# Last attention block: five score banks instead of three, and VectorE adds its running sum from key tile 4 on

## The reference, cut to what matters

```python
def _L0_xattn_ref(kv, q, Wq, bq, Wk, bk, Wv, bv, Wo, bo):   # q: 4096 x 512, kv: 3202 x 512, 16 heads of 32
    ...
    scores = jnp.einsum('bhqd,bhkd->bhqk', qh, kh) * scale
    mask = jnp.arange(Lkv)[None, :] <= jnp.arange(Lq)[:, None]
    scores = jnp.where(mask[None, None], scores, -jnp.inf)
    attn = jax.nn.softmax(scores, axis=-1)
    out = jnp.einsum('bhqk,bhkd->bhqd', attn, vh)
    ...
    return out @ Wo.T + bo
...
x = x + _L0_xattn_ref(ctx_1024, _layernorm(x, axis=-1), ...)
x = x + _L0_ffn_ref(_layernorm(x, axis=-1), ...)
```

## Time and profile before

| | |
|---|---|
| median of 3 runs | 2925.99 us (2920.41 to 2928.67) |
| the profiled execution | 2921.6 us, of which the span of the profile is 2920.0 us |
| granted TensorE clock over the span | 0.981 |
| PE busy | 2830.9 us, 97% |
| DVE busy | 1871.1 us, 64% |
| ACT busy | 1522.3 us, 52% |
| POOL busy | 1427.7 us, 49% |
| software DMA queue (POOL's) | 226.77 MB, 33.0% of 16 engines |

### The profile page before, as it was taken

The page is one execution under the profiler, slowest core; times in us unless marked ns, Lnnn a source line. Parts: engine busy times, 40 slices in busy tenths (PEclk is TensorE's granted clock), DMA queues, the critical chain, the costliest instruction groups (busy, mean ns, idle before and its releaser), DMA issues. The chain is left out here.

```text
span 2920.0 us, 42983 instructions
## 1 busy us (share of the span) xinstructions
PE 2830.9 (97%) x15944; PEld 1669.4 (57%) x15944; DVE 1871.1 (64%) x3483; ACT 1522.3 (52%) x2904; POOL 1427.7 (49%) x657
## 2 busy tenths in 40 slices
PE   8989999999999999999999999999898999999996
PEld 7877555554555554555554555553486566556653
DVE  4467888885778775778775778870463544444544
ACT  3232456666566666566667566666424434444332
POOL 0000266778566778566778566778671201111110
PEclk9998899999999999999999999999999999999998
DMA  6558456668746678746668746667694100111000
GB/s 241 189 192 250 120 142 148 148 152 187 181 131 151 157 159 190 183 129 154 154 157 191 172 128 142 142 160 190 172 331 137 58 15 30 44 44 44 30 29 15
DMA packets 138711, 407.95 MB, mean 140 GB/s; under 512 B 11632, under 2 KB 28528, under 8 KB 111888
## 3 DMA queue, kind: packets, MB, share of 16 engines
q0 software_dynamic: 32272, 226.77, 33.0%
q1 hardware_dynamic: 101056, 169.07, 20.1%
q10 hardware_dynamic: 5184, 9.44, 1.0%
HBM read 114.33 MB, written 70.78 MB: 63 GB/s over the span
## 5 line engine op out<-in xcount | busy, mean ns | idle before, releaser
L1046 ACT ACTIVATE pT<-s_bank 128x512 f32<-128x512 f32 (+5 forms) x2176 | 1086.7, 578 | 647.9 <-PE s_bank L1215 470.5
L1063 DVE TENSOR_REDUCE row_max<-m_bank 128x1 f32<-128x512 f32 (+4 forms) x2240 | 1254.1, 624 | 265.5 <-PE m_bank L1168 173.0
L986 POOL TENSOR_TENSOR part_sum<-part_sum,pT 128x2048 f32<-128x2048 f32 x192 | 889.0, 4630 | 121.2 <-ACT pT L1046 116.7
L1215 PE MATMUL s_bank<-q_sb,k_sb 104*128 104x512 f32 (+3 forms) x2176 | 839.1, 411 | 11.6 <-ACT pT L1046 7.6
L1168 PE MATMUL m_bank<-k_sb,q_sb 96*128 96x512 f32 (+4 forms) x2240 | 843.0, 410 | 7.5 <-POOL max_terms L958 2.5
L1168 PEld LDWEIGHTS m_bank<-k_sb,q_sb 96*128 96x128 f32 x2240 | 432.4, 196 | 204.8 <-DVE row_max L1063 126.5
L1215 PEld LDWEIGHTS s_bank<-q_sb,k_sb 104*128 104x128 f32 x2176 | 410.3, 192 | 208.2 <-ACT pT L1046 122.5
L1232 PE MATMUL o_bank<-pT,v_sb 128*32 128x512 f32 (+5 forms) x4352 | 499.0, 576 | 0.0
L986 POOL TENSOR_TENSOR part_sum<-pT 128x2048 f32<-128x2048 f32 x28 | 127.7, 4560 | 304.6 <-ACT pT L1046 156.8
L1232 PEld LDWEIGHTS o_bank<-pT,v_sb 128*32 128x32 f32 (+1 forms) x4352 | 113.4, 110 | 229.9 <-ACT pT L1046 115.2
L1641 POOL TENSOR_TENSOR f_var_eps<-f_mean_var,eps 128x4 f32<-128x4 f32 x8 | 1.6, 202 | 473.8 <-DVE f_mean_var L1860 473.8
(11 more groups left out here) (198 smaller groups left out, 3423.7 us busy)
## 6 DMA issues: line engine op xcount, KB each, us to landing
moved_sum<-pT POOLq DMA_DIRECT2D x208, 1024.0 KB, 7.4
q_sb<-qT_hi SPq DMA_DIRECT2D x64, 256.0 KB, 5.0
k_sb<-kT_hi SPq DMA_DIRECT2D x48, 256.0 KB, 8.3
x_in<-in_x SPq DMA_DIRECT2D x8, 1024.0 KB, 6.1
qT_hi<-q_hi SPq DMA_DIRECT2D x8, 1024.0 KB, 4.2
qT_lo<-q_lo SPq DMA_DIRECT2D x8, 1024.0 KB, 6.5
q_sb<-qT_lo SPq DMA_DIRECT2D x32, 256.0 KB, 4.7
aT<-o_sb ACTq DMA_DIRECT2D x32, 256.0 KB, 5.1
```

The lines of the kernel that those rows point to most:

```text
L986: pool.tensor_tensor(total, pT[:, slot(S - 1), :, q0:] if j and kt == 1 else total, pT[:, slot(S), :, q0:], ALU.add).then_inc(pool_added, 1)
L1046: act.activation(pT[0:rows, slot(S), h, q0:], s_bank[(HG * S + h) % S_RING][0:rows, q0:], ACT.Exp, scale=SCALE).then_inc(exp_done, 1)
L1063: dve.tensor_reduce(row_max[:, j % 2, r, h, c:c + 1], m_bank[p % M_BANKS][:, 0:n], AX_X, ALU.max).then_inc(unit_max, 1)
L1215: mm = pe.matmul(out[:, q0:], k_sb[0:R_END, h, at:at + P], q_sb[query_buffer(g, j)][0:R_END, h, q0:], start=True, stop=kt < 4 * j)
```

## The change

The scores of the last block go round five banks: the three `s_bank`s and two of the maxima's ring, which wait for the last two jobs that used them. From the block's fourth score on a score has no bank to wait for but its own; from the sixth it waits for the Exp of the score five before it. The planner knows of it. `LAST_ADDS` falls from 18 to 4, so that DVE also makes the adds of tiles 5, 7, 9, 11, 13, 15 and 17; POOL keeps those of tiles 1 and 3, the eleven transfers of the block and the multiplication of block 6's output. Nothing is changed in what is moved by DMA, nor in any other block.

```diff
 S_RING, M_BANKS = 3, 4
+LAST_RING = S_RING + 2
...
-LAST_ADDS = 18
+LAST_ADDS = 4
...
+LAST_SCORE = HG * (len(ALL_STEPS) - key_tiles(QB - 1))
+
+
+def score_before(n):
+
+    if n < LAST_SCORE + S_RING:
+        return n - S_RING
+    return n - LAST_RING if n >= LAST_SCORE + LAST_RING else None
...
     def score(self, x, S, h):
-        pe = max(x.pe, x.exp_end[0] + T_TO_WRITE) + turn + self.score_time(j, kt)
+        before = score_before(x.n)
+        pe = max(x.pe, x.exp_end[before - x.n] + T_TO_WRITE if before is not None else 0) + turn + self.score_time(j, kt)
...
+        def score_bank(n):
+
+            if n < LAST_SCORE:
+                return s_bank[n % S_RING]
+            k = (n - LAST_SCORE) % LAST_RING
+            return s_bank[(LAST_SCORE + k) % S_RING] if k < S_RING else m_bank[(len(BANK_JOBS) - S_RING + k) % M_BANKS]
...
-                        act.activation(pT[0:rows, slot(S), h, q0:], s_bank[(HG * S + h) % S_RING][0:rows, q0:],
+                        act.activation(pT[0:rows, slot(S), h, q0:], score_bank(HG * S + h)[0:rows, q0:],
                                        ACT.Exp, scale=SCALE).then_inc(exp_done, 1)
...
                     n = HG * S + h
-                    reach(pe, exp_done, max(0, n - S_RING + 1))
-                    out = s_bank[n % S_RING]
+                    before = score_before(n)
+                    if before is None:
+                        bank_free(len(BANK_JOBS) - S_RING + n - LAST_SCORE)
+                    else:
+                        reach(pe, exp_done, max(0, before + 1))
+                    out = score_bank(n)
```

More of the change, by code:

```diff
@@ L756, in best @@
     def best(self):
-        kept = [State(0, 0, 0, "scores", 9, 0, 0, 0, (0,) * S_RING, (), (0,) * M_BANKS, 0, 0, 0, None)]
+        kept = [State(0, 0, 0, "scores", 9, 0, 0, 0, (0,) * LAST_RING, (), (0,) * M_BANKS, 0, 0, 0, None)]
         for _ in range(self.scores + self.pairs + len(self.left)):
```

## The result

The changed kernel takes 2912.32 us in the median of 7 runs (2910.48 to 2914.89), the kernel before 2922.82 us in the median of 7 on the same chip. The ratio is 0.9957, 95% interval 0.9947 to 0.9967: faster by 12.6 us (9.6 to 15.5) by the ratio, 10.5 us by the medians. Forecast were 9.0 us: 2917.0 us against the 2925.99 us that the kernel before had in its first three runs. The profiled execution takes 2912.32 us, its span is 2910.7 us; it was to be 2912.6 us. All ratios here use executions at the usual speed alone: one of experiment 4 (3098 us) and two of experiment 5 (7074 and 10895 us) were far slower and don't count.

A forecast was written before the change was run, and what follows sets the result against it. Three chains (PE/ACT, POOL, DMA) bound the last block, already ending with its transfers. Tile 6 issued at 2010.7 plus 7.0 plus 42.4 gave 2060.1, denominators 9.8 us sooner, less 0.8: 9.0 us, 2917.0 us; range 2910 to 2926.

The forecast's parts named there:

- the forecast's own case: Last block ends with its accumulating transfers: 9.0 us less, 2917.0 us, own range 2914 to 2922, chance 0.66.
- rival (A): Last block: transfers stay hidden, pace 4.3 us a pair, denominators 14 us sooner, 2912 us; chance 0.13.
- The pace: Last block: accumulating transfers land 5.3 us apart, range 5.1 to 5.7; eight spacings make 42.4 us.
- The start: Start of the last block: tile 6's transfer is issued at 2010.7 (2009.2 to 2012.5) instead of 2017.41.
- step (1): Start of the last block: two more banks bring block 6's values and denominators 1 to 3 us sooner, 2 taken.
- The cost set against the change: Start of the last block: DVE's add of tile 5 slows POOL's multiplication by 0 to 2.29 us, 1 us taken.
- The 0.8 us for denominators at half clock: End of the last block: PE stands still 4 us, denominators run at half clock longer; 0.8 us off the gain.
- (B): Last block: transfers go one at a time, POOL's descriptors wait for DVE; spacing 7.0 us, 2929.6 us; chance 0.08.
- (C): Last block: PE's clock at 1.2 GHz, 7.1 us a pair, 13.6 us more, 2940 us; chance 0.06.
- (D): Nothing gained: different planner order, no sooner start, or losses after the block; 2923 to 2926 us; chance 0.07.
- the third chain: Last block: the accumulating DMA transfers, 5.2 us of all engines each, one per pair; the change removes none.

The follow-up runs named there:

- experiment 4: The full change with tiles 20 and 22 added by DVE instead of moved by transfer; 0.9958 of the kernel before.
- experiment 5: The full change once more, unaltered; 0.9963 of the kernel before, median 2914.34 us.
- experiment 3: The full change with the last block's nine accumulating transfers made plain copies, their sum left out; 0.9938 of the kernel before, median 2903.14 us.
- experiment 8: The full change with tile 22 alone added by DVE instead of moved; 0.9944 of the kernel before, median 2907.19 us.
- experiment 1: The five banks alone on the kernel before, adds of tiles 5 to 17 left on POOL; 0.9995, median 2920.73 us.
- experiment 6: The full change with DVE's adds of the last block cut to 8 of 512 queries per head; 0.9968 of the kernel before.
- the last two of 9: The full change, POOL waiting for DVE's subtraction in one output-projection block, DVE adding tiles 20 and 22, or 14, 20 and 22; 0.9945 and 0.9940.
- experiment 9: Full change, POOL waiting for DVE's subtraction in one output-projection block; DVE adding tile 22; 20 and 22; 14, 20 and 22: 0.9954, 0.9945, 0.9940.

## Why the prediction was right

**The number.** 2912.3 us is below the 2914 to 2922 us of the forecast's own case, inside the whole range (2910 to 2926), and it's the time that rival (A) gives, 2912. So the number doesn't tell which mechanism is right; the waits and the experiments do. That the profiled execution meets its 2912.6 us to 0.3 us is luck: the block gained 11.7 us instead of 9.8, and 1.7 of them were taken back ahead of the block by differences of the execution. Of the 4.7 us between 2917.0 and 2912.3, 3.2 come from the first three runs of the kernel before, whose median was 2925.99 and is 2922.82 over seven.

**What bounds.** That the block already ended with its transfers, 0.8 us behind PE, and that after the change it would end with them alone, is shown by the DMA's 5.66 us in front of the denominators and by experiments 3 and 8: take away the accumulation's time or one transfer, and the end moves at once by 6.9 and 4.7 us.

**The pace.** Forecast 5.3 us from landing to landing, measured 5.3. The chain from the issue of tile 6 to the last landing is 49.5 us, forecast 7.0 + 42.4 = 49.4. PE's and ACT's own pace was 4.44 us instead of 4.3; that is hidden.

**The start** is the term that was mis-sized. Tile 6 is issued 33.3 - 24.8 = 8.5 us sooner; forecast was 6.7. The denominators of block 6 come 14.4 - 11.0 = 3.4 us sooner, not 2 as in step (1). Of these, 1.3 us are the values right in front of them: 3.17 us before, 1.92 after. The windows view there, before and after:

```profile
1995.50:1998.50 3.00, 3.00 (x21) 0.73 (x24) 0.00 (x0) 0.68 (x2) 3.00 (x1) 0.58 0.91 345
```

```profile
1995.00:1997.00 2.00, 2.00 (x21) 0.67 (x24) 0.00 (x0) 2.00 (x5) 1.30 (x1) 1.00 1.03 383
```

The granted clock was 0.58 there before, mostly the 1.2 GHz level, and is 1.00, the 2.4 GHz level, after. Step (1) reckons with Exps alone and has no term for this. Experiment 4 shows its price: its profile has the slow values again, and tile 6 is issued 26.5 us behind the reference point instead of 24.8, which is 6.8 us sooner than before, as forecast. So nearly all that the start gained beyond the forecast is a slow stretch that this profile happens not to have. Both profiles with three banks have it, and two of the eleven with five banks (experiments 1 and 4); whether the banks make it rarer, and how often unprofiled executions have it, isn't shown. The cost set against the change, 1 us for L1011 waiting beside DVE's add, didn't come: the two collided, but DVE lost and had time. POOL then waited 0.74 us for the Exps of tile 6, so 1 us in front of that would have moved the issue by 0.3 us at most, an estimate.

**Behind it.** The 0.8 us for denominators at half clock were 0.2 us: before, they had already run cold. The total by the profiles' own stretches, block and denominators, is 11.7 - 0.2 = 11.5 us against a forecast of 9.0; the ratio's interval, 9.6 to 15.5 us, holds 11.5 and not 9.0, and the medians' 10.5 lie between the two.

**The rivals.** (A) needed transfers that overlap or hide: PE's wait of 5.66 us for a landing, the DMA share of 0.99 and experiment 3 exclude it. (B) is excluded by experiment 6. (C): the granted clock was 1.00 from 2012 to 2054, and below that only while PE stood idle at the end (0.97 over 2012 to 2060); no cost. (D) was real in kind, not in size for this kernel. Against the full change's first profile, experiments 1, 4 and 8 lost 2.4 to 2.8 us in the output projection, where POOL's add started ahead of DVE's subtraction; experiments 3 to 6 and the last two of 9 took 2.0 to 2.4 us more in the feed-forward part. The text had "instruction loads and clock stretches" in mind; the first loss is a collision of two engines with a clock stretch behind it, the second isn't explained.

**Still open.** Which way that race falls in a kernel's unprofiled runs can't be read from medians; with one profile for each kernel its share in the ratios of experiments 1, 4, 8 and 9 stays open, and so does the share of the 2.3 us in the feed-forward part and of the slow values in front of block 6's denominators. What the wait of experiment 9 is worth in the total isn't settled.

## What to carry to other kernels

When several chains run at nearly the same pace, price each one before the change: here they beat at 5.5, 5.4 and 5.2 us. Neither half of the change gave anything in the total that could be measured (0.9995, 0.9997), both together gave 0.9957, and the third chain then set both the end and the next gain. Look at the stretch that was changed, too, and not only at the total: in the profiles the banks alone had shortened the block by 4.6 us and the adds alone by nothing. The larger part of the gain, 8.5 of 11.7 us, was how much sooner the first link of the remaining chain could start; 3.2 came from its links following each other more closely. Before a difference of starts is put down to the change, compare the granted clock in front of them: 1.7 us of this one come and go with the clock. Once the chain is known, move single links of it to the engine that has become idle: three tiles from DMA to DVE brought the block from 74.3 to 67.5 us.

## What the runs showed of the hardware

An accumulating transfer of 1.05 MB within SBUF held all 16 DMA engines for 5.2 us (nine in 48 us at 97.7%) and landed after 7.0 us as the first of its row; a plain copy of the same size landed after 4.4 to 5.1 us, and once after 6.0 (experiment 3). The cost of the accumulation, not of the bytes, set the end of the block.

DVE instructions with two inputs from SBUF and POOL adds or multiplications held each other up: on DVE 3.87 us for an add of 2.29 (beside 1.28 us on POOL), 1.78 for one of 0.19, 3.38 for a subtraction of 2.28. In the output projection 0.1 us decided which of them waited. POOL's transfer issues were not held by DVE's adds: with adds of 0.19 us instead of 2.29 the block was the same to 0.1 us. Nor did an issue that fell into an add stretch it: such adds took 2.29 us.

The same 16 value matmuls took 1.92 us at a granted clock of 1.00 and 3.2 to 3.6 us at 0.51 to 0.58, and the slow case came in some executions and not in others with the same instructions up to there (experiments 4 and 5).
